# Decoder kernel, first stage: an unsliced prefix ratio, the second normalisation's result on ScalarE, and another place for the recurrence's transposes

## The reference, cut to what matters

```
# recurrence, on x
gate_x, gate_a = sigmoid(x @ w_in + b_in), sigmoid(x @ w_a + b_a)     # block-diagonal
a      = minimum(exp(-gate_a * (softplus(a_param) + 0.001)), 1 - 1e-5)
n      = x * gate_x * sqrt(maximum(1 - a*a, 1e-5))
prefix = maximum(concat([1, cumprod(a)[:-1]]), 1e-7)      # along the 128 positions
h      = prefix * cumsum((n + 1e-7) / prefix)
x      = layernorm(x + h)                                 # x1
# retention against the context, positions turned and scaled (xpos)
q, k, v = xpos(x @ Wq), xpos_inverse(ctx @ Wk), ctx @ Wv
x      = layernorm(x + (q @ k.T * decay) @ v)             # x2
```

## Time and profile before

| | us |
|---|---|
| median of 3 runs | 1653.03 |
| the runs | 1653.03, 1653.17, 1645.95 |
| profiled execution, its own time | 1644.63 |
| its span, first to last instruction | 1642.8 |
| PE busy | 1518.9 (92%) |
| DVE busy | 1130.2 (69%) |
| ACT busy | 802.5 (49%) |
| POOL busy | 580.0 (35%) |
| TensorE clock granted, mean | 0.977 |

### The profile page before, as it was taken

How to read it: one execution, slowest core, us unless ns; L and a number is a source line. 1 busy time by engine, 2 the same in 40 slices (tenths; PEclk the granted TensorE clock), 3 DMA queues, 4 the chain that set the end, 5 groups by cost and what they waited for, 6 DMA issues and landing times.

```text
span 1642.8 us, 34390 instructions
## 1 busy us (share of the span) xinstructions
PE 1518.9 (92%) x12742; PEld 1354.4 (82%) x12742; DVE 1130.2 (69%) x2350; ACT 802.5 (49%) x1527; POOL 580.0 (35%) x684
## 2 busy tenths in 40 slices
PE   4888888899999999888889799999989999989997
PEld 2777777799999999777777588888879999989997
DVE  3899987756655655227888558877867767766674
ACT  5777742244544454235676544545434444443442
POOL 3666650212111210047777212111104444443443
PEclk9999999899999999989999899999999999999999
DMA  5222253212333321062323141222134463554443
GB/s 190 65 78 77 70 192 122 78 44 86 97 97 102 102 97 33 27 211 70 98 79 112 52 160 56 66 66 62 44 74 99 100 132 83 117 113 86 108 91 66
DMA packets 118159, 152.11 MB, mean 93 GB/s; under 512 B 10090, under 2 KB 102852, under 8 KB 117508
## 3 DMA queue, kind: packets, MB, share of 16 engines
q1 hardware_dynamic: 110068, 127.48, 28.1%
q0 software_dynamic: 6560, 19.02, 4.0%
q10 hardware_dynamic: 1392, 3.70, 0.6%
HBM read 111.37 MB, written 38.80 MB: 91 GB/s over the span
## 4 chain that ended last, share of the span: by engine, by line
PE 47%; ACT 5%; issue 2%; DVE 2%; DMA 1%; POOL 0%; SPq 0%; ACTq 0%; POOLq 0%; DVEq 0%
PE psum L531 21%; PE psum L1861 4%; PE psum L1449 4%; PE psum L1845 3%; PE psum L498 3%; PE psum L506 3%; PE psum L1839 2%; PE psum L1822 2%; ACT arena_y L1549 1%; PE psum L490 1%; PE psum L2209 1%; ACT arena_y L1566 1%; PE psum L1496 1%; PE psum L1481 1%; ACT arena_y L1403 1%
## 5 line engine op out<-in xcount | busy, mean ns | idle before, releaser
L2189 POOL TENSOR_TENSOR d_g_parts<-arena_w,d_g_parts 128x512 fp32r<-128x512 f32 x128 | 165.3, 1291 | 249.1 <-ACT d_g_parts L2321 249.1
L531 PE MATMUL psum<-d_v_high,d_g_parts 128*128 128x256 f32 x1024 | 203.9, 283 | 3.0 <-DVE arena_x L1979 2.9
L531 PE MATMUL psum<-d_x_parts,d_v_high 128*128 128x256 f32 x1024 | 193.8, 287 | 7.6 <-issue 6.1
L531 PE MATMUL psum<-m_w_high,m_h_parts 128*128 128x256 f32 x1024 | 188.0, 284 | 0.0
L1213 ACT ACTIVATE arena_x<-psum,b_e 128x512 f32<-128x512 f32 x128 | 88.3, 690 | 189.6 <-PE psum L531 89.6
L531 PEld LDWEIGHTS psum<-d_x_parts,d_v_high 128*128 128x128 f32 x1024 | 159.2, 191 | 14.6 <-issue 8.4
L1141 POOL DMA_INDIRECT arena_x<-x_d,slot_row x64 | 67.1, 1049 | 293.3 <-PE psum L1187 229.1
L531 PEld LDWEIGHTS psum<-d_v_high,d_g_parts 128*128 128x128 f32 x1024 | 167.5, 190 | 3.7 <-issue 3.0
L2329 ACT ACTIVATE arena_y<-psum 128x512 f32<-128x512 f32 x128 | 76.4, 597 | 182.8 <-PE psum L531 182.7
L531 PE MATMUL psum<-m_xF_parts,m_w_high 128*128 128x512 f32 x512 | 159.8, 394 | 2.1 <-DVE m_xF_parts L526 2.1
L531 PEld LDWEIGHTS psum<-m_w_high,m_h_parts 128*128 128x128 f32 x1024 | 160.7, 192 | 0.0
(11 more groups left out here) (281 smaller groups left out, 3644.0 us busy)
## 6 DMA issues: line engine op xcount, KB each, us to landing
arena_x<-wT_d SPq DMA_DIRECT2D x128, 256.0 KB, 5.4
arena_y<-in_L_ffn_w SPq DMA_DIRECT2D x16, 1024.0 KB, 8.0
x_d<-arena_x SPq DMA_DIRECT2D x32, 256.0 KB, 2.2
y_d<-arena_x SPq DMA_DIRECT2D x16, 512.0 KB, 9.0
arena_x<-kv_d SPq DMA_DIRECT2D x16, 512.0 KB, 3.3
kv_d<-arena_x SPq DMA_DIRECT2D x9, 512.0 KB, 2.9
arena_x<-in_x SPq DMA_DIRECT2D x16, 256.0 KB, 2.9
arena_x<-in_ctx SPq DMA_DIRECT2D x16, 256.0 KB, 3.0
```

What stands on the lines that cost most here:

```text
L531: ins = nc.tensor.matmul(dst, left[a_], right[b_], start=start and k == 0, stop=stop and k == 2, skip_group_check=True)
L2189: nc.gpsimd.tensor_tensor(K["gP"][:, s % 4, 1], K["g"][:, s % 2], K["gP"][:, s % 4, 0].bitcast(F32), ALU.subtract).then_inc(d_gl, 1)
```

## The change

Three edits, all in the first stage.

First, the ratio. It was written in four runs of 127 elements at an offset of one element; a cell of zero at the start of each run was set once. Now one instruction over 512 elements writes the whole tile `A["ratio"]`, unshifted. A second one, behind a wait for the first, sets the last element of each run to zero (MEMSET of 4 elements a partition), and the scan reads the tile from one element earlier. The semaphore a_r counts 2 a unit instead of 1.

Second, the normalisation that ends with x2. DVE computed (r2 - mean) * rstd. Now DVE prepares variance + eps and -mean (two small instructions instead of one), POOL computes rstd and -mean * rstd (two instead of one), and ACT computes r2 * rstd + shift in two ACTIVATEs at the end of its step, behind the copy of x. The functions for this, ln_shift, root_and_shift and ln_result, stood in a later stage already and are moved up. DVE now waits for ACT's result of the unit before, where it writes r2.

Third, the four transposes of r1. They stood at the start of PE's step, for unit u3. Now they stand behind the projection of v (L689) in the step ahead, for the same unit, which is u2 there, and ahead of the transposes of context and x.

```diff
--- before.py
+++ after.py
@@ -483,6 +483,30 @@
             done(pool, s_ag, u)
             nc.gpsimd.tensor_tensor(stats[:, :, 8:9], stats[:, :, 9:10], minus_half[:, :, :], ALU.pow).then_inc(s_rs, 1)
 
+        def ln_shift(dve, u, stats, sems):
+
+            done(dve, sems[0], u, 2)
+            done(dve, sems[2], u.back(1), 2)
+            nc.vector.tensor_scalar(stats[:, :, 9:10], stats[:, :, 7:8], LN_EPS, None, ALU.add)
+            nc.vector.tensor_scalar(stats[:, :, 10:11], stats[:, :, 6:7], -1.0, None, ALU.mult).then_inc(sems[1], 1)
+
+        def root_and_shift(pool, u, stats, sems):
+
+            done(pool, sems[1], u)
+            done(pool, sems[3], u.back(1))
+            nc.gpsimd.tensor_tensor(stats[:, :, 8:9], stats[:, :, 9:10], minus_half[:, :, :], ALU.pow).then_inc(sems[2], 1)
+            pool.wait_ge(sems[2], u.n * 2 + 1)
+            nc.gpsimd.tensor_tensor(stats[:, :, 11:12], stats[:, :, 10:11], stats[:, :, 8:9],
+                                    ALU.mult).then_inc(sems[2], 1)
+
+        def ln_result(act, u, src, dst, stats, sems):
+
+            done(act, sems[2], u, 2)
+            for b in range(UB):
+                ins = nc.scalar.activation(dst[:, b, :], src[:, b, :], ACT.Identity, scale=stats[:, b, 8:9],
+                                           bias=stats[:, b, 11:12])
+            ins.then_inc(sems[3], 1)
+
         def to_feature(dst, src):
 
             for c in range(NC_):
@@ -549,15 +573,17 @@
             A[n] = arena_x.take([P, 2, NC_, T])
         A["qp"] = arena_x.take([P, 2, NC_, T])
         A["qr"] = arena_x.take([P, 2, NC_, T])
-        for n in ("u", "r", "t1", "t2"):
+        for n in ("u", "t1", "t2"):
             A[n] = arena_x.take([P, NC_, T])
+        PAD = 8
+        A["ratio"] = arena_x.take([P, PAD + NC_ * T])
         for n in ("x1", "x2", "v"):
             A[n] = arena_x.take([P, 2, UB, D])
         arena_y.reset(12800)
         A["r2"] = arena_y.take([P, UB, D])
         A["sc"] = arena_y.take([P, 2, UB, S])
         A_st1 = sb("A_st1", [P, UB, 10])
-        A_st2 = sb("A_st2", [P, UB, 10])
+        A_st2 = sb("A_st2", [P, UB, 12])
 
         a_in, a_inc, a_cst = sem2("a_in"), sem2("a_inc"), sem2("a_cst")
         aT_x, aT_c, aT_r1, aT_x1, aT_x2 = (sem("aT_" + n) for n in ("x", "c", "r1", "x1", "x2"))
@@ -617,15 +643,7 @@
                 return ins
 
             def step(t):
-                u0, u1, u3, u4, u5, u6 = (t.at(k, UNITS) for k in (0, 1, 3, 4, 5, 6))
-                if u3:
-                    done(pe, a_r1, u3)
-                    done(pe, a_x1F, u3.back(1))
-                    for b in range(UB):
-                        for c in range(NC_):
-                            ins = nc.tensor.transpose(bank(1)[:, b * D + c * P:b * D + (c + 1) * P],
-                                                      A["r1"][:, u3.p, c, b * S:(b + 1) * S], ident)
-                    ins.then_inc(aT_r1, 1)
+                u0, u1, u2, u3, u4, u5, u6 = (t.at(k, UNITS) for k in range(7))
                 if u5:
                     done(pe, a_qr, u5)
                     done(pe, a_kr, u5)
@@ -690,6 +708,14 @@
                                                    A["cF"][:, u4.p, c, b * S:(b + 1) * S],
                                                    w["L0_xattn_Wv"][:, c, :], start=(c == 0), stop=(c == NC_ - 1))
                     ins.then_inc(a_v, 1)
+                if u2:
+                    done(pe, a_r1, u2)
+                    done(pe, a_x1F, u2.back(1))
+                    for b in range(UB):
+                        for c in range(NC_):
+                            ins = nc.tensor.transpose(bank(1)[:, b * D + c * P:b * D + (c + 1) * P],
+                                                      A["r1"][:, u2.p, c, b * S:(b + 1) * S], ident)
+                    ins.then_inc(aT_r1, 1)
                 if u3:
                     landed(pe, a_inc, u3)
                     if u1:
@@ -711,7 +737,7 @@
             act.wait_ge(a_init, 2)
 
             def step(t):
-                u0, u1, u2, u3, u4, u6 = (t.at(k, UNITS) for k in (0, 1, 2, 3, 4, 6))
+                u0, u1, u2, u3, u4, u5, u6 = (t.at(k, UNITS) for k in range(7))
                 if u2:
                     done(act, a_min, u2)
                     done(act, a_mg, u2.back(2))
@@ -731,7 +757,7 @@
                                                    bias=hgate_b[:, c:c + 1], scale=0.5)
                     ins.then_inc(a_thx, 1)
                     done(act, a_tha, u1)
-                    done(act, a_r, u1.back(2))
+                    done(act, a_r, u1.back(2), 2)
                     done(act, a_sq, u1.back(2))
                     for c in range(NC_):
                         ins = nc.scalar.activation(A["a"][:, u1.p, c, :], A["tha"][:, u1.p, c, :], ACT.Exp,
@@ -769,6 +795,10 @@
                     done(act, aT_x, u0)
                     done(act, a_r1, u0.back(2))
                     nc.scalar.activation(A["xF"][:, u0.p], chunks(bank(2)), ACT.Copy).then_inc(a_xF, 1)
+                if u5:
+                    done(act, aT_x2, u5.back(2))
+                    landed(act, a_st, u5.back(2))
+                    ln_result(act, u5, A["r2"], A["x2"][:, u5.p], A_st2, ln2)
             pipelined(act, UNITS, A_LAG, step)
 
         def a_vector(dve):
@@ -795,7 +825,9 @@
                 if u2:
                     p = u2.p
                     flat = {n: A[n][:, p].rearrange("p c t -> p (c t)") for n in ("inv", "h")}
-                    flat |= {n: A[n].rearrange("p c t -> p (c t)") for n in ("u", "r")}
+                    flat["u"] = A["u"].rearrange("p c t -> p (c t)")
+                    flat["a"] = A["a"][:, p].rearrange("p c t -> p (c t)")
+                    ratio, ratio_before = A["ratio"][:, PAD:], A["ratio"][:, PAD - 1:PAD - 1 + NC_ * T]
                     done(dve, a_thx, u2)
                     done(dve, a_mg, u2.back(2))
                     nc.vector.scalar_tensor_tensor(A["g"][:, p], A["thx"][:, p], 1.0, A["xF"][:, p], ALU.add,
@@ -807,8 +839,9 @@
                     done(dve, a_u, u2)
                     done(dve, a_min, u2)
 
-                    nc.vector.tensor_tensor(quads(A["r"])[:, :, 1:S], quads(A["a"][:, p])[:, :, 0:S - 1],
-                                            quads(A["u"])[:, :, 0:S - 1], ALU.max).then_inc(a_r, 1)
+                    nc.vector.tensor_tensor(ratio, flat["a"], flat["u"], ALU.max).then_inc(a_r, 1)
+                    dve.wait_ge(a_r, u2.n * 2 + 1)
+                    nc.vector.memset(ratio.rearrange("p (n s) -> p n s", s=S)[:, :, S - 1:S], 0.0).then_inc(a_r, 1)
                 if u5:
                     done(dve, a_score, u5)
                     done(dve, a_ret, u5.back(2))
@@ -820,11 +853,12 @@
                     xpos(bank(5), "xpos_k_cos", "xpos_k_sin", A["t1"], A["t2"], a_kt)
                 if u2:
                     done(dve, a_xe, u2)
-                    done(dve, a_r, u2)
-                    nc.vector.tensor_tensor_scan(flat["h"], flat["r"], flat["h"], 0.0, ALU.mult,
+                    done(dve, a_r, u2, 2)
+                    nc.vector.tensor_tensor_scan(flat["h"], ratio_before, flat["h"], 0.0, ALU.mult,
                                                  ALU.add).then_inc(a_h, 1)
                 if u5:
                     done(dve, a_ret, u5)
+                    done(dve, a_x2, u5.back(1))
                     nc.vector.tensor_tensor(A["r2"][:, :, :], seqs(bank(6)), A["x1"][:, u5.p],
                                             ALU.add).then_inc(a_r2, 1)
                 if u3:
@@ -833,7 +867,9 @@
                     ln_apply(dve, u3, seqs(bank(1)), A["x1"][:, u3.p], A_st1, ln1)
                 if u5:
                     done(dve, a_r2, u5)
-                    ln_stats(dve, u5, A["r2"], A_st2, ln2)
+                    ln_bn(dve, u5, A["r2"], A_st2, ln2)
+                    ln_moments(dve, u5, A_st2, ln2)
+                    ln_shift(dve, u5, A_st2, ln2)
                 if u4:
                     done(dve, a_q, u4)
                     done(dve, a_qr, u4.back(1))
@@ -846,14 +882,10 @@
 
                     nc.vector.tensor_scalar(A["inv"][:, u1.p], A["inv"][:, u1.p], 1.0 / (1.0 - A_EPS), None,
                                             ALU.max).then_inc(a_cap, 1)
-                if u5:
-                    done(dve, aT_x2, u5.back(2))
-                    landed(dve, a_st, u5.back(2))
-                    ln_apply(dve, u5, A["r2"], A["x2"][:, u5.p], A_st2, ln2)
 
             for p in range(2):
                 nc.vector.memset(quads(A["inv"][:, p])[:, :, 0:1], BIG).then_inc(a_init, 1)
-            nc.vector.memset(quads(A["r"])[:, :, 0:1], 0.0).then_inc(a_init, 1)
+            nc.vector.memset(A["ratio"][:, 0:PAD], 0.0).then_inc(a_init, 1)
             dve.wait_ge(a_init, 3)
             pipelined(dve, UNITS, A_LAG, step)
 
@@ -886,7 +918,7 @@
                     nc.gpsimd.tensor_tensor(kr[:, 0, :], A["t1"][:, 0, :], A["t2"][:, 1, :], ALU.add)
```

(20 more changed lines are left out.)

## The result

The changed kernel took 1665.96 us in the median of 4 runs (1663.09 to 1672.31), the kernel before 1649.49 in the median of 4. The ratio is 1.012, with a 95% interval of 1.0089 to 1.015: slower by 16.5 us in the medians and by some 20 by the ratio. Predicted was 1659, from a sum of +6.9, with 0.50 for no difference and 0.42 for slower; the direction was right, the size about two and a half times too small. The profiled execution took 1663.09, 18.5 more than that of before.

The account below looks back on a forecast made before the run. DVE set the pace before; afterwards a loop through ScalarE and GpSimd was to bind at 14.29 us a step. Ten steps +5.5, step 16 to 17 +0.3 and filling +1.1 made +6.9, giving 1659 us, range 1646 to 1667.

Parts of the forecast that it names:

- Loop A: First-stage dependency loop through ScalarE and GpSimd: 13.18 us of a 13.74 step before, 14.29 and binding after.
- The sum: Links of the lengthened first-stage loop add to 14.29, 14.23 in the mean step against 13.68; in all +6.9 us.
- Filling: First steps of the first stage: moved transposes of r1 delay x1's transposes in step 5 by 1.1 us, bounds 0 and 2.
- The end: Behind step 17 of the first stage: nothing on ACT late, x2's transposes behind other matmuls, so 0.
- The ratio: DVE's ratio instruction: 0.92 of 1612 ns is a stall from POOL, the offset costs nothing, the added MEMSET 0.1.
- R1: POOL's L871 or L874 meets a two-SBUF-input DVE instruction again: 3.8 us more, +10.7, 1664; chance 0.22.
- R4: A cheaper ACT pair and no loss in filling: +2 to +4 us, 1656; with near nothing, chance 0.15.
- R2: Faster: ACT's pair or r1's transposes find cover, a 13.13 loop decides; -4.4 us, 1648.6; chance 0.15.
- R3: The unshifted ratio tile is itself faster, the stall was the offset's; DVE's work 11.9, time as forecast; no chance given.
- The range: Whole kernel time from 1646 to 1667 us; the forecast's own part 1654 to 1664.
- Loop B: First-stage loop through PE and DVE, x1's transposes, gates, k's projection and scan: 13.13 us a step, not binding.
- DVE's list: DVE's own work per first-stage step after the change: 12.8 us, 11.9 if the ratio's stall goes; not binding.

Follow-up runs that it names:

- experiment 3: Changed kernel plus 16 idle identity transposes on TensorE ahead of its wait for x1 in steady steps; 1.0061 against the kernel before.
- experiment 10: Changed kernel plus 16 idle transposes ahead of the wait for x1, and r1's transposes at their old place in steps 3 and 4; 1.0038 against the kernel before.
- experiment 5: Changed kernel with ScalarE's pair ahead of the copy of v and r1's transposes at the old place in steps 3 and 4; 0.9990 against the kernel before.
- experiment 4: Changed kernel with ScalarE's pair for x2 ahead of the copy of v instead of behind the copy of x; 1.0012 against the kernel before.
- Experiment 9: Kernel before with the new ratio alone (one 512-wide instruction plus MEMSET), normalisation and transposes as before; 1.0029 against the kernel before.
- experiment 6: Changed kernel with ScalarE's pair ahead of the copy of v and r1's transposes at the old place in every step; 1.0005 against the kernel before.
- experiment 8: Changed kernel with the pair ahead of v's copy, r1's old transposes in steps 3 and 4, 8 idle transposes before the x1 wait; 0.9986 against the kernel before.
- experiment 11: As experiment 8, with 24 more idle transposes in step 3 and 12 in step 4; 0.9987 against the kernel before.
- experiment 1: Changed kernel with the second normalisation's result back on VectorE, ratio and r1's transposes as changed; 1.0007 against the kernel before.
- experiment 2: Changed kernel with r1's four transposes back at the start of TensorE's step, ratio and ScalarE's pair as changed; 1.0016 against the kernel before.
- experiment 7: Changed kernel with r1's transposes at their old place in steps 3 and 4 only; 1.0081 against the kernel before.

## Why the prediction was off, point by point

- **Loop A.** Right. Its slack was 0.56, the added 0.41 and 0.99 and the returned 0.32 gave 14.29 in a step like that of rows 3; measured 14.34. The link from L689 to the context's copy came to 2.97, not 2.94: rows 3 have a hand-over of 0.06 there (149.66 to 149.72), and the sum took 0.03. DVE's wait at the scan, the square right behind L506 and the ratio ahead of L903 came as forecast.
- **The sum, "Loop A after: ... 14.29", is the step that failed.** It carried L689's link over from rows at full clock and priced TensorE's longer wait at nothing. I even listed that wait as a sign of being right. From 0.70 to 2.18 us, it let the clock fall in four of ten steps, 1.6 to 1.8 us each, and the mean step was 15.0, not 14.23. Experiments 3 and 10 fill the wait and leave the loop: 1.0061 and 1.0038.
- **Filling.** +1.1 with bounds 0 and 2; measured +2.4. The transposes there delay as said (experiment 5), but the copy of x in step 3 comes at 44.38, 1.8 later and not 1.4, and the sum's "one transfer" on the way to 44.0 is 1.2 us for which no row stands. The rows in between are at the lower clock: four transposes take 0.87 there (41.55 to 42.42), where the sum had 0.44. The granted clock is 0.57, 0.50 and 0.56 in the three stretches of ten from 20 to 50 us, and 1.00, 0.92 and 0.74 before; how much of the 2.4 is the clock's is not separated.
- **The end.** Taken as 0; measured +3.1. With idle transposes (experiment 10) it is 271.44 - 236.28 = 35.2, and as much in experiment 3, so 1.0 without the clock and 2 by the clock.
- **The ratio.** Right that the new tile is worth nothing and that the stall is a meeting with GpSimd. The MEMSET was priced at 0.1, and where DVE binds the step is 0.25 longer with it; in the changed kernel DVE waits anyway.
- **R1 to R4.** L906 had 1.04, so R1 was wrong, and R2 would have needed the pair elsewhere, which is experiment 4. Experiment 9 refutes R3, and for R4 the pair would have had to be cheaper than its 0.98. None of the rivals was the clock.
- **The range.** 1665.96 lies within 1646 to 1667, but by luck: the upper end was there for R1 and for the scatter of the runs, and the forecast's own range ended at 1664.
- **Loop B and DVE's list** were not the whole of what binds next: loop B itself came to 13.36 (experiment 4), not 13.13, and with the pair hidden and the old transposes a third loop gave 13.93 (experiment 6).

How the changed kernel's cost divides, by the experiments: with the old filling and the idle transposes +0.38%, the moved transposes in the filling up to +0.23% more (1.0061 against 1.0038), the clock from step 5 on +0.6% (1.012 against 1.0061). The intervals are 0.3 to 0.6% wide from end to end, so the last two are rough.

The Trainium skill, "TensorE: Matmul & The Clock Gate", section "HAM oscillation — how this bites in real kernels", describes a kernel in which TensorE waits for a DMA in every tile and starts again at half the clock. The rows here agree in that a projection behind a wait can be at the lower clock, 3.50 against 1.97 behind 2.18; but the wait is for another engine, and it happens in four steps of ten.

## What to carry to other kernels

An instruction moved to an engine with half its time idle is free only at a place where that engine is idle; ask which loop runs through the link it is put in, and how much slack that loop has, before adding up busy time. When a loop gets longer, ask too what TensorE's wait in it becomes: a wait that grows may cost twice, once as itself and once in the matmuls behind it. If the wait can't go, a few idle transposes in it are a cheap test. Here they took back about half of the loss (1.0061 for 1.012); where the wait was 1.2, no gain in time could be told.

## What the runs showed of the hardware

- One profiled execution of each kernel, the projections of v in steps 6 to 16, eleven each: with waits for x1 of 0.3 to 0.7 us, no projection was slow (seven kernels: the one before, experiments 3, 6, 8, 9, 10 and 11); with 1.2 to 1.7, one in each of experiments 1, 2 and 4 and two in experiment 5; with 2.1 to 2.2, four in the changed kernel and five in experiment 7 (step 6 has a shorter wait in some). TensorE's other waits in a step were not held equal.
- Transposes of the identity, with no reader, kept the clock up in a wait of 2.18 us (experiment 3: 1.97 for each projection).
- A one-element offset in SBUF cost an instruction of VectorE nothing (0.69 in rows 4); who starts first, it or GpSimd, cost 0.92.
- The record of the clock can fail: in experiment 3 it has 1.00 from 20 to 50 us, while the gates there take 3.78, at the lower level.

```profile
34.07 3.78 PE L666 MATMUL psum<-arena_x,arena_w 128*128 128x256 f32 x8 [0.69 <-ACT arena_x L800]
...
145.23 1.99 PE L666 MATMUL psum<-arena_x,arena_w 128*128 128x256 f32 x8
```
